# Query statistics, key norms and the query load: three reorderings in an attention loop

## The reference, cut to what matters

```python
qx = _fp8_linear_pertensor(ln_out, wqx, ...).reshape(b, s, g, hpg, d)
qx = _ln(qx, qxln_w, qxln_b)
kvx = jnp.einsum('bsi,oi->bso', cond, w_kv_x)
kx, vx = jnp.split(kvx, 2, axis=-1)
kx = _ln(kx.reshape(b, sc, g, d), kxln_w, kxln_b)
xout = _gqa(qx, kx, vx.reshape(b, sc, g, d))      # softmax(q k / sqrt(d)) v
```

## Time and profile before

| | |
|---|---|
| median of three runs | 2188.6 us (2184.24 to 2190.7) |
| the profiled execution | 2188.6 us, span of its trace 2187.3 us |
| TensorE busy | 1976.7 us, 90% of the span |
| weight loads busy | 1667.4 us, 76% |
| VectorE, ScalarE, Pool busy | 1154.9, 938.6, 654.7 us |
| the 64 iterations of attention | about 190 to 1790 us of the span |
| iterations without refill | 24.4 and 25.2 us in turn, from `exp_bias` to `exp_bias` |
| mean time of one: matmul spacing in `keys`, transpose L519, `q_f` L726 | 0.18, 0.27, 0.40 us |

### The profile page before, as it was taken

The page is one execution under the profiler, slowest core; times in us unless marked ns, Lnnn a source line. Parts: engine busy times, 40 slices in busy tenths (PEclk is TensorE's granted clock), DMA queues, the critical chain, the costliest instruction groups (busy, mean ns, idle before and its releaser), DMA issues. The chain is left out here.

```text
span 2187.3 us, 30639 instructions
## 1 busy us (share of the span) xinstructions
PE 1976.7 (90%) x10424; PEld 1667.4 (76%) x10424; DVE 1154.9 (53%) x2672; ACT 938.6 (43%) x1787; POOL 654.7 (30%) x707
## 2 busy tenths in 40 slices
PE   3899999999999999999999999999999984758758
PEld 3678888888888888888888888888888873631536
DVE  6564454445444554455344545454554435968854
ACT  4554354444433443444344434443443434617321
POOL 3224543222233223222222322233223213510331
PEclk9999999999999999999999999999999996879769
DMA  6675344434332433344333434343432226400020
GB/s 193 198 235 162 116 141 124 153 92 143 114 119 82 141 118 116 103 142 132 103 116 116 134 89 129 111 149 91 141 118 82 77 67 216 191 21 3 1 77 20
DMA packets 213130, 255.73 MB, mean 117 GB/s; under 512 B 62120, under 2 KB 132392, under 8 KB 212464
## 3 DMA queue, kind: packets, MB, share of 16 engines
q1 hardware_dynamic: 202480, 252.92, 37.1%
q10 hardware_dynamic: 8448, 0.43, 0.2%
q0 software_dynamic: 2048, 0.43, 0.1%
HBM read 222.32 MB, written 30.83 MB: 116 GB/s over the span
## 5 line engine op out<-in xcount | busy, mean ns | idle before, releaser
L478 PE MATMUL kx_ps<-ctxT_hi,wk_hi 128*128 128x400 f32 (+1 forms) x1024 | 375.6, 367 | 10.0 <-DVE ctxT_lo L288 8.7
L482 PE MATMUL kx_ps<-ctxT_hi,wk_lo 128*128 128x400 f32 (+1 forms) x1024 | 361.3, 353 | 0.0
L480 PE MATMUL kx_ps<-ctxT_lo,wk_hi 128*128 128x400 f32 (+1 forms) x1024 | 360.3, 352 | 0.0
L564 PE MATMUL u_ps<-ctxN_hi,pt_hi 128*128 128x512 f32 (+1 forms) x832 | 341.9, 411 | 3.3 <-DVE pt_lo L760 3.3
L565 PE MATMUL u_ps<-ctxN_lo,pt_hi 128*128 128x512 f32 (+1 forms) x832 | 330.4, 397 | 0.0
L566 PE MATMUL u_ps<-ctxN_hi,pt_lo 128*128 128x512 f32 (+1 forms) x832 | 329.2, 396 | 0.0
L698 DVE TENSOR_TENSOR kx_lo<-kx_ps,kx_hi 128x400 fp32r<-128x400 f32 (+1 forms) x256 | 146.8, 574 | 307.4 <-ACT sq L938 307.4
L760 DVE TENSOR_TENSOR pt_lo<-t_ps,pt_hi 128x512 fp32r<-128x512 f32 (+1 forms) x256 | 145.2, 587 | 294.4 <-ACT pt_hi L971 294.2
L936 ACT ACTIVATE kx_hi<-kx_ps 128x400 fp32r<-128x400 f32 (+1 forms) x256 | 129.2, 505 | 394.7 <-PE kx_ps L482 391.7
L971 ACT ACTIVATE pt_hi<-t_ps 128x512 fp32r<-128x512 f32 (+1 forms) x256 | 126.7, 529 | 324.4 <-PE t_ps L548 324.2
L478 PEld LDWEIGHTS kx_ps<-ctxT_hi,wk_hi 128*128 128x128 f32 x1024 | 198.7, 194 | 13.2 <-DVE ctxT_lo L288 9.0
(11 more groups left out here) (248 smaller groups left out, 3640.8 us busy)
## 6 DMA issues: line engine op xcount, KB each, us to landing
rstd_bc<-scratch_rstd SPq DMA_DIRECT2D x64, 804.0 KB, 5.7
stage<-in_ctx_t SPq DMA_DIRECT2D x96, 267.0 KB, 4.7
stage<-in_ctx_n SPq DMA_DIRECT2D x96, 256.0 KB, 6.1
wk_hi<-scratch_wk_s SPq DMA_DIRECT2D x56, 256.0 KB, 2.8
wk_lo<-scratch_wk_s SPq DMA_DIRECT2D x56, 256.0 KB, 3.1
wv_hi<-scratch_wv_s SPq DMA_DIRECT2D x56, 256.0 KB, 4.0
wv_lo<-scratch_wv_s SPq DMA_DIRECT2D x56, 256.0 KB, 4.7
scratch_own_rows<-out_sb SPq DMA_DIRECT2D x32, 256.0 KB, 3.0
```

Source lines behind the costliest of these rows:

```text
L478: PE.matmul(kx_ps[:, j % 2, 0:w], wk_hi[:, g % 2, i, :], ctxT_hi[:, i, c0:c0 + w], start=(i == 0), stop=False)
L480: PE.matmul(kx_ps[:, j % 2, 0:w], wk_hi[:, g % 2, i, :], ctxT_lo[:, i, c0:c0 + w], start=False, stop=False)
L482: mm = PE.matmul(kx_ps[:, j % 2, 0:w], wk_lo[:, g % 2, i, :], ctxT_hi[:, i, c0:c0 + w], start=False, stop=(i == C - 1))
L564: PE.matmul(u_ps[:], pt_hi[0:w, t % 2, cols], ctxN_hi[0:w, y, :], start=(y == 0), stop=False)
```

## The change

Three operations change their place. Nothing is added or left out.
- VectorE: `query_stats(n+2)` moves from between `query_low(n+1)` and `scale_scores(n+1, 0)` to behind `softmax_bias(n+1)`. It is still left out at n = -1 and where there is no query n+2.
- Pool: `key_rstd(n+2)` moves ahead of `query_norm(n+2)`.
- SP: `load_query` of a query is issued one iteration later, in the same iteration as its statistics; queries 0 and 1 are loaded earlier, as before.

```diff
--- before.py
+++ after.py
@@ -878,8 +878,6 @@
                 if s:
                     if v:
                         query_low(n + 1)
-                        if r:
-                            query_stats(n + 2)
                     scale_scores(n + 1, 0)
                     scale_scores(n + 1, 1)
                 if v:
@@ -890,6 +888,8 @@
                     scale_scores(n + 1, 2)
                     scale_scores(n + 1, 3)
                     softmax_bias(n + 1)
+                if v and r:
+                    query_stats(n + 2)
                 refill(3)
                 if k:
                     keys_low(n + 3, 0)
@@ -1175,10 +1175,10 @@
                     split_wv(n)
                 if 3 <= n + 3 < G_:
                     x.split_wk(n + 3)
+                if n + 2 < N:
+                    key_rstd(n + 2)
                 if 2 <= n + 2 < N:
                     query_norm(n + 2)
-                if n + 2 < N:
-                    key_rstd(n + 2)
                 if odd and u + 1 < N // 2:
                     own_norm(u + 1)
 
@@ -1317,8 +1317,8 @@
                 if n >= 0 and g == 1 and b < B - 1:
                     for k in range(RING):
                         x.load(b + 1, k)
-                if 2 <= n + 3 < N:
-                    load_query(n + 3)
+                if 2 <= n + 2 < N:
+                    load_query(n + 2)
                 if 1 <= n + 1 < G_:
                     load_wv(n + 1)
                 if 3 <= n + 4 < G_:
```

## The result

The change made the kernel slower: 2238.6 us (median; 2236.8 to 2241.0) against 2189.7 us for the kernel before, ratio 1.0229 with a 95% interval of 1.0208 to 1.025.

A forecast was written before the change was run, and what follows sets the result against it. TensorE was taken to bound the attention stage, its busy time and waits filling it. Late-query stalls of 31 x 1.45 + 16 x 1.15 + 2.0 = 65.4 us on 2188.6 gave 2254 us, range about 2240 to 2272.

The forecast's parts named there:

- What bounds the kernel, and where the stall stands: Attention stage: TensorE sets the time; q_n, loadable 2.53 us after exp_bias starts, comes late and TensorE waits for it.
- The exposed stalls, 45.0 + 18.4 + 2.0: TensorE loses 1.45 us in 31 even iterations, 1.15 in 16 odd ones, and 2.0 at n = 61.
- The 14 cost nothing: In 14 odd refill iterations the 1.15 us stall only shortens TensorE's existing q_f wait at row_term: cost 0.
- The rival of the falling clock: Regular gaps bring TensorE's mean granted clock to 0.80 in the stage: 374 us more, about 2630 us; chance 0.02.
- Edit 3 at 0: SP queue: issuing load_query one iteration later costs 0.
- Edit 2 at 0: Pool: key_rstd ahead of query_norm runs in Pool's idle time, margin 1.87 us, and costs 0.
- without this edit the held-back `key_rstd` would be hidden too: Pool: key_rstd held back until the late query would cost nothing, its result being needed some 20 us later.
- The hidden rival: TensorE catches up within 14% headroom beside its weight loads, so the time stays at 2188.6 us; chance 0.04.
- The range: Whole kernel: about 2240 to 2272 us around the forecast of 2254, from handoffs, empty array, stats start and run spread.

The follow-up runs named there:

- e8: Kernel before with query_stats late only in the 14 odd refill iterations and key_rstd ahead of query_norm on Pool: 2173.7 us, ratio 0.9926.
- e6: Full change with query_stats one step further back on VectorE, behind keys_low(n+3, 0): 2428.8 us, ratio 1.1093 to the kernel before.
- e7: Full change without the later load_query, which stays one iteration ahead: 2239.3 us, ratio 1.0226 to the kernel before.
- e2: Kernel before with only the Pool and SP parts of the change, query_stats where it was: 2190.0 us, ratio 1.0001.
- e1: Kernel before with only query_stats moved behind softmax_bias, Pool's and SP's order as before: 2284.8 us, ratio 1.0434.
- e5: Full change with VectorE's refill(4) also moved behind query_out: 2233.7 us, ratio 1.0202 to the kernel before.
- e4: Kernel before with only VectorE's refill(4) moved behind the output copies and query_out: 2153.4 us, ratio 0.9834.

## Why the prediction was wrong in size and right in kind

- **What bounds the kernel, and where the stall stands: right.** TensorE could load `q_n` 2.55 us behind `exp_bias` in all but the 14 odd refill iterations (forecast 2.53), and it waited for it in every iteration with a query. The recorded waits are 1.22 us in even iterations and 0.9 in odd ones without refill, as forecast.
- **The exposed stalls, 45.0 + 18.4 + 2.0: nearly right.** From the distances between loads of `q_n` in the two traces, an even iteration lost 1.31 us and an odd one without refill 1.23, together 2.54 where 2.60 was forecast. 31 x 1.31 + 16 x 1.23 + 2.0 = 62.3 us, 3.1 less than forecast.
- **"The 14 cost nothing": this is the step that failed.** The term was put at 0 and measured 1.8 - 16.6, some 15 us of gain. The stall there was covered, as the step said, though it was longer than the 1.15 us forecast: Pool is slower beside VectorE's work on the context pieces (`q_ve` 0.58 us instead of 0.24), `q_n` was loaded 3.2 us behind `exp_bias`, and so 1.86 us late. The `q_f` wait behind it took that up; the load of `row_term` stands where it stood, to 0.05 us. Counted between loads of `q_n`, 0.13 us were left, 14 x 0.13 = 1.8 us. But cutting the 2 us wait into two kept the clock up, and this gave back 16.6 us: it is what remains of the 47.5 us by which the last `row_term` is later than the first ones, 62.3 + 1.8 - 16.6.
- **The same gain, read directly.** From `row_term` to the next load of `q_n`, which waits in its turn, the changed kernel takes 1.5 us longer at n = 5, 31 and 47, where the clock hadn't fallen before. At the 11 places where it had, this 1.5 us is paid back: 9 of them have the distance of before to 0.12 us, n = 39 is 0.3 us longer, and n = 7 is 1.5 us shorter, where a wait of 1.4 us for `pt_lo` went as well. That is about 18 us, less 1.6 us for the one fall at n = 40. So some 15 of the 16.6 us are the clock, and 1.4 that wait. Among these 14 iterations only those with a fall gained. e8 shows about the same amount by itself, 16 us. The remaining 2 us of the difference between the spans lie in front of and behind the stage, and their cause is open.
- **Why I missed it.** I had the row: a mean granted clock of 0.99 in the earlier trace rows was read as "gaps of this length do nothing". It is a mean over 1575 us, and its missing hundredth was the term. I put the clock into a rival that could only make things worse, and never asked which waits of the kernel before already cost clock, and so what it would bring to break one up. Windows of 1 us behind the `q_f` waits would have shown 0.50 in 11 of 14.
- **The rival of the falling clock** was held to be ruled out for gaps of up to 2.0 us; the trace of the kernel before says the opposite, as its clock fell behind 11 of these very gaps. The rival hardly came with this change, whose waits stay at 1.6 us or less up to n = 60, with one fall, but e6 shows it at waits 1.6 us longer, for 93 us.
- **Edit 3 at 0: right** (e7). **Edit 2 at 0: right by itself** (e2), but the sentence beside it, that without this edit the held-back `key_rstd` would be hidden too, was wrong by 46 us (e1). I had followed `load_rstd` to its own reader, 20 us later, and not the context loads that stand behind it in SP's queue.
- **The hidden rival** (14% of headroom by the share of weight loads) fell: e5 against e4 shows the full 80 us. Here the sum of busy time and waits was the better witness.
- **The range** took the uncertainty of each term, 0 to 0.3 us for a handoff, and had no place for a term that was missing. (Its lower steps, 3, 5 and 4 us, lead from 2254 to 2242, put down as about 2240.)

## What to carry to other kernels

On an engine that has no idle time but its waits, as TensorE here, a chain that is delayed costs its lateness in every iteration in which no later wait takes it up; find the moment at which the consumer needs it and compare, for each kind of iteration. Then look at the granted clock in short windows behind each wait that the kernel already has, not at its mean over the stage: a wait of 2 us cost 1.5 us more in half-speed matmuls where the clock fell, and two waits of 1.5 and 0.3 us cost only themselves. Behind a late instruction, follow every queue to its end: what stands behind the waiting transfer cost 45.5 us here, while the reader of that transfer comes some 20 us later.

## What the runs showed of the hardware

- TensorE's granted clock went to 0.50 for some 3 us behind recorded waits of 2.0 us in 11 of 14 places (9 of 14 in e2), and in none of the 14 where the same time was cut into about 1.5 and 0.3 us, neither in the changed kernel nor in e7 or e8. In the changed kernel it went down once, behind the single wait of 1.57 us of n = 40; in e6, with waits of 2.6 to 3.8 us, behind 53 of 61. TensorE was "busy" throughout, with 10 matmuls in 3 us instead of 22.
- Pool's small operations take longer while VectorE computes the low halves of context pieces (`ctxT_lo`, L288): `q_ve` takes 0.57 or 0.58 us in the 14 odd refill iterations of the changed kernel and 0.24 or 0.25 in the others. The cause was not tested.
- The recorded idle time of TensorE is less than the time lost (0.90 against 1.23 us in odd iterations without refill); the record of the matmul ahead reaches into the gap, and the row of weight loads has 1.30 us at the same place.
